# Gate coefficient from PSUM, a gate weight handed over in three pieces, and unit 0 prepared sooner

## The reference, cut to what matters

```
d = w - mean;  coeff = mean(|d|) over the whole 1792 x 512 matrix;  W = mean + coeff * sign(d)
gate = xn @ W1.T;  up = xn @ W3.T;  h = silu(gate) * up;  g = silu(h @ W2.T)
out = x + s * g
```

## Time and profile before

| | us |
|---|---|
| three runs | 534.46, 534.47, 535.68 (median 534.47) |
| profiled execution, time | 534.48 |
| profiled execution, span of the instructions | 532.7 |
| PE busy | 519.8 (98%) |
| DVE busy | 443.0 (83%) |
| ACT busy | 328.5 (62%) |
| POOL busy | 94.6 (18%) |
| granted TensorE clock, mean | 0.999 of full |

### The profile page before, as it was taken

The page is one execution under the profiler, slowest core; times in us unless marked ns, Lnnn a source line. Parts: engine busy times, 40 slices in busy tenths (PEclk is TensorE's granted clock), DMA queues, the critical chain, the costliest instruction groups (busy, mean ns, idle before and its releaser), DMA issues.

```text
span 532.7 us, 6530 instructions
## 1 busy us (share of the span) xinstructions
PE 519.8 (98%) x2352; PEld 432.1 (81%) x2352; DVE 443.0 (83%) x520; ACT 328.5 (62%) x455; POOL 94.6 (18%) x106
## 2 busy tenths in 40 slices
PE   4999999999999999999999999999999999999997
PEld 3778888888888888888888888888888888888886
DVE  6989998988896988865898888999999898874447
ACT  2979978557546655446648557968776585464310
POOL 1311002003100310022003121300310040004491
PEclk9999999999999999999999999999999999999999
DMA  8999905045711491059228994941592387127503
GB/s 337 394 401 404 385 8 168 15 137 98 197 54 46 76 234 49 1 106 223 56 70 160 250 217 90 186 101 40 109 187 47 74 163 144 36 46 161 135 20 139
DMA packets 31745, 76.73 MB, mean 144 GB/s; under 512 B 3873, under 2 KB 7297, under 8 KB 31585
## 3 DMA queue, kind: packets, MB, share of 16 engines
q1 hardware_dynamic: 21632, 57.42, 34.4%
q0 software_dynamic: 9792, 18.88, 20.5%
q10 hardware_dynamic: 288, 0.02, 0.0%
HBM read 53.23 MB, written 2.10 MB: 104 GB/s over the span
## 4 chain that ended last, share of the span: by engine, by line
PE 95%; DVE 3%; DMA 1%; issue 0%; ACT 0%; SPq 0%
PE up_ps L1726 28%; PE gate_pair L1726 27%; PE down_pair L1767 11%; PE up_ps L1767 9%; PE down_ps L1767 7%; PE side_ps L1810 2%; PE down_pair L1726 2%; PE down_pair L1677 1%; PE up_ps L1887 1%; PE gate_pair L1887 1%; PE down_pair L1887 1%; DMA xn<-in_x 1%; PE down_pair L1849 1%; PE gate_pair L1767 1%; PE down_pair L1782 1%; DVE xn L1135 1%
## 5 line engine op out<-in xcount | busy, mean ns | idle before, releaser
L1726 PE MATMUL up_ps<-xT,gu 128*128 128x512 f32 x648 | 151.9, 390 | 0.0
L1726 PE MATMUL gate_pair<-xT,gu 128*128 128x512 f32 x624 | 148.4, 390 | 0.9 <-DVE gu L1175 0.9
L1726 PEld LDWEIGHTS up_ps<-xT,gu 128*128 128x128 f32 x648 | 121.6, 188 | 25.1
L1726 PEld LDWEIGHTS gate_pair<-xT,gu 128*128 128x128 f32 x624 | 117.2, 188 | 25.4 <-DVE gu L1175 1.4
L655 POOL DMA_DIRECT2D y<-y_part x64 | 55.4, 878 | 338.3 <-ACT y_part L819 337.1
L806 ACT ACTIVATE h<-up_ps 128x512 fp32r<-128x512 f32 x52 | 31.1, 597 | 110.1 <-DVE up_ps L1242 57.0
L865 ACT ACTIVATE ramp<-codes,bend_bias 128x1536 f32<-128x1536 uint8 x56 | 88.1, 1580 | 1.9 <-DVE acc L1350 1.6
L1350 DVE SCALAR_TENSOR_TENSOR acc<-ramp,acc 128x1536 f32<-128x1536 f32 x42 | 73.6, 1753 | 4.9 <-ACT ramp L865 4.3
L1767 PE MATMUL down_pair<-h,dn 128*128 128x512 f32 x249 | 60.9, 390 | 0.0
L1767 PEld LDWEIGHTS down_pair<-h,dn 128*128 128x128 f32 x249 | 46.8, 188 | 9.8
L1247 DVE TENSOR_TENSOR h<-up_ps,h 128x512 fp32r<-128x512 f32 x52 | 35.8, 688 | 19.7 <-ACT h L806 19.4
(11 more groups left out here) (227 smaller groups left out, 647.2 us busy)
## 6 DMA issues: line engine op xcount, KB each, us to landing
y<-y_part POOLq DMA_DIRECT2D x64, 256.0 KB, 5.1
scale<-in_scales SPq DMA_DIRECT2D x28, 384.0 KB, 5.5
scan_w<-in_w SPq DMA_DIRECT2D x15, 512.0 KB, 11.0
base<-in_mean SPq DMA_DIRECT2D x9, 768.0 KB, 4.4
scan_mean<-in_mean SPq DMA_DIRECT2D x9, 512.0 KB, 10.1
silu_gate<-in_mean SPq DMA_DIRECT2D x6, 512.0 KB, 12.4
codes<-in_codes SPq DMA_DIRECT2D x14, 192.0 KB, 6.0
xn<-in_x SPq DMA_DIRECT2D x4, 512.0 KB, 5.0
```

Of the source, the lines that this page charges most:

```text
L1726: last = nc.tensor.matmul(ps[:, :], w[:, w_part, hc * P:(hc + 1) * P], xT[:, x_part, hc, th * HALF:(th + 1) * HALF], start=(hc == 0 and w_ ...
```

## The change

`ones` is filled with 1/(1792*512) instead of 1, so `side_ps` holds the coefficient itself. `split_make` reads it there as its scalar; `take_coeff` is now a copy without a scale (`keep_coeff`) and a wait, and for GATE the copy stands after the third `split_make` and the second `split_low`. Chunk 1's gate weight is handed over in three pieces of 128, 128 and 256 columns, and PE waits before hc 0, 1 and 2. `early_high` stands ahead of `scan_signs(0)`, `early_low` no longer waits for the second scan difference (the wait now stands behind it), and `unit_subtract(1)` no longer waits for the low parts of four x tiles. `unit_high(3)` stands ahead of `scan_signs(5)`.

```diff
+PIECES = [(0, P), (P, 2 * P), (2 * P, HID)]
...
-            nc.gpsimd.memset(ones[:], 1.0).then_inc(const_ready, 1)
+            nc.gpsimd.memset(ones[:], 1.0 / (INTER * HID)).then_inc(const_ready, 1)
...
             def early_low():
                 pool.wait_ge(gu_hi, 1)
-                pool.wait_ge(scan_diff, dve_tiles(1))
...
             early_low()
+            pool.wait_ge(scan_diff, dve_tiles(1))
             unit_subtract(0)
-            pool.wait_ge(xT_lo, 4)
             unit_subtract(1)
...
             x_high(3)
+            early_high()
             scan_signs(0)
-            early_high()
...
-            split_high(0)
-            split_high(1)
+            for n in range(len(PIECES)):
+                split_high(n)
...
             silu(1, 0)
+            unit_high(3)
             scan_signs(5)
-            unit_high(3)
...
+            def keep_coeff(m):
+                dve.wait_ge(total_ready, m + 1)
+                nc.vector.tensor_copy(coeff[:, m:m + 1], side_ps[:, m:m + 1]).then_inc(coeff_ready, 1)
+
             def take_coeff(m):
-                dve.wait_ge(total_ready, m + 1)
-                nc.vector.tensor_scalar(coeff[:, m:m + 1], side_ps[:, m:m + 1], 1.0 / (INTER * HID), None, ALU.mult
-                                        ).then_inc(coeff_ready, 1)
+                keep_coeff(m)
                 dve.wait_ge(coeff_ready, m + 1)
...
             take_part(GATE)
-            take_coeff(GATE)
             split_make(0)
             split_make(1)
             split_low(0)
+            split_make(2)
             split_low(1)
+            keep_coeff(GATE)
+            split_low(2)
+            dve.wait_ge(coeff_ready, 1)
             early_scale(0)
...
-                    if hc == HC // 2 and k == SPLIT_UNIT and kind == GATE and th == 0:
+                    if hc == 1 and k == SPLIT_UNIT and kind == GATE and th == 0:
+                        pe.wait_ge(piece_lo, 2)
+                    if hc == 2 and k == SPLIT_UNIT and kind == GATE and th == 0:
                         pe.wait_ge(gu_lo, gu_count(k, kind))
```

More of the change, by code:

```diff
@@ L360, in block_kernel @@
         unit_made = sem("unit_made")
-        half_made = sem("half_made")
-        half_hi = sem("half_hi")
-        half_lo = sem("half_lo")
+        piece_made = sem("piece_made")
+        piece_hi = sem("piece_hi")
+        piece_lo = sem("piece_lo")
         early_part = sem("early_part")
@@ L739, in unit_signs, with split_high @@
                 nc.scalar.activation(unit_raw(u), unit_raw(u), ACT.Sign).then_inc(unit_sign, 1)
[L741 to L744, removed]
+            def split_high(n):
+                sl = slice(*PIECES[n])
+                if n < 2:
+                    act.wait_ge(piece_made, n + 1)
                 else:
@@ L747, in split_high @@
                 nc.scalar.activation(unit_split(SPLIT_UNIT)[:, HI, sl], unit_base(SPLIT_UNIT)[:, sl], ACT.Copy
-                                     ).then_inc(half_hi if half == 0 else gu_hi, 1)
+                                     ).then_inc(piece_hi if n < 2 else gu_hi, 1)
             def unit_high(u):
@@ L1160, in unit_make, with split_make, split_low @@
                                                ALU.mult, ALU.add).then_inc(unit_made, 1)
-            def split_make(half):
-                sl = slice(half * HID // 2, (half + 1) * HID // 2)
+            def split_make(n):
+                sl = slice(*PIECES[n])
                 dve.wait_ge(unit_sign, SPLIT_UNIT + 1)
+                dve.wait_ge(total_ready, GATE + 1)
                 nc.vector.scalar_tensor_tensor(unit_base(SPLIT_UNIT)[:, sl], unit_raw(SPLIT_UNIT)[:, sl],
[L1166 to L1172, removed]
+                                               side_ps[:, GATE:GATE + 1], unit_base(SPLIT_UNIT)[:, sl], ALU.mult, ALU.add
+                                               ).then_inc(piece_made if n < 2 else unit_made, 1)
+            def split_low(n):
+                sl = slice(*PIECES[n])
+                if n < 2:
+                    dve.wait_ge(piece_hi, n + 1)
                 else:
@@ L1176, in split_low @@
                                         unit_split(SPLIT_UNIT)[:, HI, sl].bitcast(f32), ALU.subtract
-                                        ).then_inc(half_lo if half == 0 else gu_lo, 1)
+                                        ).then_inc(piece_lo if n < 2 else gu_lo, 1)
             def unit_low(u):
@@ L1699, in project @@
                 if k == SPLIT_UNIT and kind == GATE and th == 0:
-                    pe.wait_ge(half_lo, 1)
+                    pe.wait_ge(piece_lo, 1)
                 elif kind == GATE or k <= FIRST:
```

## The result

The changed kernel takes 535.38 us in the median of 20 executions (535.13 to 536.10), the kernel before 534.51 of 20 (534.30 to 535.68): 1.0015 times the time, 95% interval 1.0008 to 1.0021. That is 0.87 us more, inside the 0.3% named as no change, and close to the forecast 535.2. With twenty executions a side the 0.87 us are clear of noise, so here is where they come from. One execution of the kernel before, 886.78 us at a mean clock of 0.561, is left out of every figure here.

A forecast was written before the change was run, and what follows sets the result against it. PE, busy 98%, bounds the kernel; at most some 1.9 us of its idle time can be won. 534.48 plus 0.76 at `total(UP)`, collision less hand-over and other shifts, gave 535.2 us; own range 534.8 to 535.8, 80% range 533.9 to 536.1.

The forecast's parts named there:

- The collision: Unit 0's `early_low` on POOL beside DVE's `normalise` near 16 us: DVE 1.1 us late, `early_mean` at 21.9.
- The hand-over: Chunk 1's gate weight at 31 us: scalar from PSUM and narrower pieces let PE start 0.87 us earlier, bounds 0.3 to 0.95.
- The sum: Both effects carried to `total(UP)`: it starts at 50.65 against 49.89, +0.76 us, and this stays to the end.
- Rival 1: POOL is kept out or harmless beside `normalise`; the order on ACT takes the hand-over's gain back: 534.5 us, chance 0.27.
- ACT's order: `unit_high(3)` ahead of `scan_signs(5)` holds ACT's sums of UP, so the part for `total(UP)` ends 0.37 us later.
- Rival 3: PE's clock falls to 1.2 GHz among the transposes before 20.81 us: +3.0 for 12 matmuls, 538.2 us, chance 0.05.
- wrong altogether: Sign against the whole forecast: a wait appears past 60 us, where no chain was followed.

## Why the prediction was right

- *The collision.* Forecast: DVE 1.1 late and `early_mean` at 21.9. Found: 0.96 and 21.86 (0.09 of it a later start). The four `normalise` take 2.87 us, not about 3.0. The price came from a row 500 us away, where DVE starts just behind POOL, and from reading `normalise` as an instruction that uses a path the PSUM readers don't. Putting the one wait back takes it all away.
- *The hand-over.* Forecast 0.87, found 0.8, with a wait of 0.21 us left on PE (forecast: under 0.2). In the lines below a piece of 128 columns costs DVE 0.36 to make, not 0.3, and `split_make(1)` starts 0.16 us behind the end of the first, so the first low part comes later than worked out.

```profile
30.50 0.36 DVE L1168 SCALAR_TENSOR_TENSOR unit_st<-unit_st,side_ps 128x128 f32<-128x128 f32 x1 [0.87 <-PE side_ps L1701]
31.02 0.35 DVE L1168 SCALAR_TENSOR_TENSOR unit_st<-unit_st,side_ps 128x128 f32<-128x128 f32 x1 [0.16 <-issue]
```

- *The sum.* Forecast +0.76 at the UP total, found +0.69, and +0.87 in the medians. `scan_subtract(5)` came free of POOL (1.21) and ACT did not wait ahead of `unit_high(3)`, both as said; the wait at the total was 0.29, not 0.5, since PE came 0.17 later than I had it and the total followed its part by 0.06, not 0.12. Part of the closeness is luck: the collision was taken 0.14 too long and the hand-over 0.07 to 0.09 too large, which offset each other on PE, and some 0.15 of the 0.87 in the medians is in no profile of the change at full clock and in no term of the forecast.
- *Rival 1*, without the collision nothing: 534.47 measured, 534.5 worked out. ACT's order, which I made responsible for 0.37 of it, is worth 0.14; most of what held PE was there already, since the kernel before has only 0.39 us of reserve at this total (49.89, less the 49.45 at which its part ends and 0.05 for the hop).
- *Rival 3*, the clock: what it describes happens, in 3 of 31 executions. Its price was mis-sized. I put the lower clock on 12 wide matmuls, +3.0 us, but it lay over transposes and warm-up ahead of them: +0.7.
- *What would have shown it wrong altogether*, a wait of PE past 60 us, is not there.

## What to carry to other kernels

A step moved earlier is not free because its engine is idle: ask whose path it lies beside in its new place. Here POOL work is harmless beside reductions and PSUM readers and costs up to its own length beside a fast SBUF-to-SBUF scale or an operation with two SBUF inputs. And before paying for a shorter wait, measure the reserve at the next appointment: 0.8 us was won, 0.39 of reserve stood behind it, and one reorder of sums on ACT (534.47 to 533.79) was worth more than the third piece, which by itself shortened nothing at the end.

## What the runs showed of the hardware

A POOL instruction that becomes ready beside back-to-back `normalise` gets in between two of them and holds DVE for most of its length (0.96 of 1.28 us). The delay is on a single `normalise`: of the eight in that execution the longest takes 1503 ns, the median 542.

```profile
L1135 DVE TENSOR_SCALAR xn<-xn,moments,inv_std x8: 511/542/1503, 8.8 to 17.6; 128x512 f32<-128x512 f32 x8
```

The Trainium skill, SBUF — State Buffer, section "Who interferes with whom", says that DVE in a two-port mode and POOL block each other for a whole instruction, and holds reductions free of it. The runs agree. In the kernel before, a reduction beside POOL takes 1.22 us and one without, at 47.96 us, 1.21. `early_add`, which reads PSUM, takes 0.69 us beside POOL at 34.79 and 0.69 without, at 32.93. POOL, then DVE:

```profile
34.55 1.47 POOL L641 TENSOR_TENSOR unit_st<-unit_st 128x512 f32<-128x512 f32 x1 [9.89 <-DMA unit_st<-in_mean]
45.05 1.30 POOL L641 TENSOR_TENSOR unit_st<-unit_st 128x512 f32<-128x512 f32 x1 [2.90 <-DVE scan_w L1095]
```
```profile
32.93 0.69 DVE L1510 TENSOR_TENSOR down_pair<-down_pair,silu_gate 128x512 f32<-128x512 f32 x1
34.79 0.69 DVE L1510 TENSOR_TENSOR down_pair<-down_pair,silu_gate 128x512 f32<-128x512 f32 x1
45.01 1.22 DVE L1101 TENSOR_REDUCE abs_sums<-scan_w 128x1 f32<-128x1024 f32 x1
```

A two-input subtraction of 1024 columns takes 1.21 us alone and is held by its overlap with POOL less some 0.1 us: 1.52, 1.72 and 2.32 us at overlaps of 0.43, 0.63 and 1.24. That a memset also delays `normalise` (0.28 us) fits the section too, since there such an instruction takes the shared write path; one profile shows it.
